# Three stages of an attention and expert layer: three blocks with barriers, or one block with waits by data

## The reference

```python
x = L0_attn_x                                   # (8, 512, 256)
xn = _layernorm(x)
# attention: 16 heads of 16, a band of 64 keys to either side
qkv = xn @ Wqkv + bqkv
scores = where(|i - j| <= 64, q @ k.T * 16 ** -0.5, -inf)
attn_out = softmax(scores) @ v @ Wout + bout
# experts: 8, hidden 1024, the top 2 of each token
logits = xn @ router_w + router_b               # gating: softmax over the top 2
h = relu(xn @ w1[e] + b1[e]);  y = h @ w2[e] + b2[e]
ffn_out = sum over the two experts of gating * y
out = x + attn_out + ffn_out
```

## Time and profile before

| | |
|---|---|
| median of 3 runs | 956.04 us (954.45 to 956.12) |
| the profiled execution's own time | 957.17 us |
| its span | 955.1 us |
| TensorE busy | 903.1 us (95%) |
| VectorE busy | 824.7 us (86%) |
| ScalarE busy | 740.7 us (78%) |
| GpSimd busy | 480.5 us (50%) |

### The profile page before, as it was taken

One profiled execution on the slowest core, in us unless ns is written; L12 is line 12 of the kernel. 1 busy time (PEld: TensorE's weight loads), 2 busy tenths in 40 slices (PEclk: granted clock), 3 DMA queues, 4 the chain that ended last, 5 costly groups with the idle time before them and its releaser, 6 DMA issues. The chain is left out here.

```text
span 955.1 us, 27555 instructions
## 1 busy us (share of the span) xinstructions
PE 903.1 (95%) x7684; PEld 876.4 (92%) x7684; DVE 824.7 (86%) x2171; ACT 740.7 (78%) x1985; POOL 480.5 (50%) x700
## 2 busy tenths in 40 slices
PE   4989799899999999999969999999999999999996
PEld 3878788889999999999969999999999999999996
DVE  5876699998888888888857999999999999999995
ACT  3545699899999999999956777777777776777773
POOL 5120013236465646555544666556666666556663
PEclk9999799999999999999998999999999999999999
DMA  4979532344444444455335222222222222221210
GB/s 143 322 268 308 169 79 75 117 122 136 136 136 135 137 135 133 136 141 148 105 87 163 37 34 44 46 36 36 34 34 43 47 49 49 35 44 35 36 22 1
DMA packets 69867, 95.33 MB, mean 100 GB/s; under 512 B 15549, under 2 KB 48960, under 8 KB 69696
## 3 DMA queue, kind: packets, MB, share of 16 engines
q1 hardware_dynamic: 52800, 77.97, 27.0%
q0 software_dynamic: 17024, 16.88, 11.2%
HBM read 62.91 MB, written 35.53 MB: 103 GB/s over the span
## 5 line engine op out<-in xcount | busy, mean ns | idle before, releaser
L1029 ACT ACTIVATE weights_qkv<-weights_qkv,low 128x256 f32<-128x256 f32 (+1 forms) x512 | 240.2, 480 | 1.1 <-DVE low L832 1.1
L1456 ACT ACTIVATE hid<-ps_experts,b_s 128x256 f32<-128x256 f32 x312 | 131.0, 473 | 117.5 <-PE ps_experts L1523 87.4
L1344 POOL DMA_INDIRECT out<-y,target x78 | 137.3, 1761 | 127.4 <-DVE y L1422 113.8
L843 DVE TENSOR_TENSOR pt<-ps_attend,pt 128x512 fp32r<-128x512 f32 (+1 forms) x256 | 158.4, 620 | 39.9 <-ACT pt L1042 39.3
L1123 PE MATMUL ps_attend<-pt,v_m 128*80 128x256 f32 (+7 forms) x1536 | 187.8, 271 | 2.3 <-DVE inv_t L856 1.8
L1539 PE MATMUL ps_experts<-w_hi,h_hi 128*128 128x256 f32 x624 | 175.4, 281 | 1.1 <-DVE h_lo L1391 1.1
L1523 PE MATMUL ps_experts<-xgt_hi,w_hi 128*128 128x256 f32 x624 | 173.7, 278 | 2.8 <-DVE xgt_lo L1382 2.8
L1123 PEld LDWEIGHTS ps_attend<-pt,v_m 128*80 128x80 f32 (+3 forms) x1536 | 171.4, 162 | 4.2 <-issue 4.2
L1523 PE MATMUL ps_experts<-xgt_hi,w_lo 128*128 128x256 f32 x624 | 173.6, 278 | 0.0
L1523 PE MATMUL ps_experts<-xgt_lo,w_hi 128*128 128x256 f32 x624 | 173.5, 278 | 0.0
L1539 PE MATMUL ps_experts<-w_lo,h_hi 128*128 128x256 f32 x624 | 172.6, 277 | 0.0
(11 more groups left out here) (174 smaller groups left out, 2008.6 us busy)
## 6 DMA issues: line engine op xcount, KB each, us to landing
weights_qkv<-in_w SPq DMA_DIRECT2D x15, 1024.0 KB, 7.1
qk_hi<-weights_qkv SPq DMA_DIRECT2D x16, 512.0 KB, 4.8
qk_lo<-weights_qkv SPq DMA_DIRECT2D x16, 512.0 KB, 5.5
q_st<-qk_hi SPq DMA_DIRECT2D x128, 64.0 KB
k_st<-qk_hi SPq DMA_DIRECT2D x128, 64.0 KB
weights_qkv<-in_x SPq DMA_DIRECT2D x8, 512.0 KB, 4.3
xn_rows<-weights_qkv SPq DMA_DIRECT2D x8, 512.0 KB, 5.2
k_st<-qk_lo SPq DMA_DIRECT2D x64, 64.0 KB
```

Of the source, the lines that this page charges most:

```text
L843: v.tensor_tensor(lo[:, f:l], ps[:, bank_t[h], 0:l - f], hi[:, f:l].bitcast(F32), ALU.subtract).then_inc(s_plo, 1)
L1029: ins = act.activation(wt[:, ring, at_tile(i)], wt[:, ring, at_tile(i)], ACT.Exp, bias=low[:, ring, i:i + 1], scale=-1.0, accum_out=total[ ...
L1344: pool.indirect_dma_start(out_tokens, bass.IndirectOffsetOnAxis(ap=target[:, h:h + 1], axis=0), y[:, h], None, bounds_check=T - 1, oob_is_ ...
L1456: ins = act.activation(hid[:, n % 2, j], ps[:, bank_h[n], j * ROWS:(j + 1) * ROWS], ACT.Relu, bias=b1[:, ds(e * FC + 2 * n + j, 1)])
```

## The change

All three stages stand in one block. There is no drain, barrier or `start` between them; the order at both seams is kept by waits on what is needed.

- Tiles of the later stages become views of F32R buffers that stay allocated: the parts of w1 lie in `q_st`, those of w2 in `v_m` and `k_st`, the projection's `w_lo` and `xt_lo`, attention's `pt` and the experts' rows and hidden layer share `work`, and so on.
- The semaphores of the later stages (65, and the two of the output stores) are raised by GpSimd at the start of the program.
- Seam 1: the scores of head 0 follow the projection; before those of head 1 TensorE waits for VectorE's last q and k part, behind those of head 2 for the logits. VectorE waits for the mask constants and the normalised rows' stores, GpSimd for v.
- Seam 2: GpSimd gathers the first rows after head 14 of the last batch. ScalarE and VectorE load the first expert's number and make w1's first half before the last inverses and values, ScalarE w1's second half after the inverses. TensorE runs the first half of the last projection, then waits for the gathered rows and transposes them, then runs the second half. The rows' parts, w1's second half on VectorE and w2's first half follow. The second and third gather each have their memset directly ahead; the third's waits for the second's landing.
- The identity is cast at the start of the program, b1 is loaded early in attention.

```diff
                                    base=0, pattern=[[-1, P]], channel_multiplier=1).then_inc(s_ident, 1)
+                start(pool, g.later.values())
+                start(pool, g.s_out)
...
+                v.wait_ge(s_ident, 2 + START)
+                v.tensor_copy(g.ident_r[:], g.ident[:])
                 statistics(0, 0)
...
-        pt = sb("pt", [P, 2, 2, SPAN], F32R)
-        a_hi = sb("a_hi", [P, DC, N], F32R)
-        a_lo = sb("a_lo", [P, DC, N], F32R)
+        pt = g.work[:].rearrange("p (r s w) -> p r s w", r=2, s=2)
+        a_hi, a_lo = g.split[:, 0], g.split[:, 1]
...
+                    sp.dma_start(g.b1[:], g.b1_cols).then_inc(s_b1, 16)
...
+                def gather_first():
+                    pool.wait_ge(s_rows, 16 + START)
+                    pool.tensor_copy(g.index[:, 0], g.rows[:, 0:2, 0].bitcast(U32)).then_inc(s_idx, 1)
+                    pool.wait_ge(s_idx, 1 + START)
+                    for h in range(2):
+                        pool.indirect_dma_start(
+                            g.first_rows[:, h].bitcast(F32), None, g.xn_dram,
+                            bass.IndirectOffsetOnAxis(ap=g.index[:, 0, h:h + 1], axis=0),
+                            bounds_check=T - 1, oob_is_err=False).then_inc(g.s_g[h], 16)
...
+                        if last and n == 14:
+                            gather_first()
+
+                pool.wait_ge(g.projection["s_vlo"], 2 * B + START)
                 batch(0, True, False)
                 batch(1, False, False)
+                pool.wait_ge(g.projection["s_table"], 16 + START)
                 with pool.Fori(2, B - 1) as b:
                     batch(b, False, False)
                 batch(B - 1, False, True)
-                pool.wait_ge(s_rows, 16 + START)
-                pool.tensor_copy(g.first_index[:], g.rows[:, 0:2, 0].bitcast(U32)).then_inc(s_first, 1)
-                pool.wait_ge(s_first, 1 + START)
-                for h in range(2):
-                    pool.indirect_dma_start(
-                        g.first_rows[:, h].bitcast(F32), None, g.xn_dram,
-                        bass.IndirectOffsetOnAxis(ap=g.first_index[:, h:h + 1], axis=0),
-                        bounds_check=T - 1, oob_is_err=False).then_inc(g.s_g[h], 16)
...
+                v.wait_ge(g.projection["s_const"], 5 + START)
+                v.wait_ge(g.projection["s_xnout"], 16 * B + START)
...
+                v.wait_ge(s_named, 1 + START)
+                first = v.value_load(g.step_expert[0:1, 0:1], min_val=0, max_val=E - 1)
+
+                def lo_of_w1(n):
+                    cols = slice(n * F // 2, (n + 1) * F // 2)
+                    v.wait_ge(s_w1hi, n + 1 + START)
+                    v.tensor_tensor(g.w1_lo[:, :, cols], g.w1_of(first)[:, :, cols], g.w1_hi[:, :, cols].bitcast(F32),
+                                    ALU.subtract).then_inc(s_w1lo, 1)
+
+                lo_of_w1(0)
                 v.wait_ge(s_pv, HC * 2 * B + START)
                 v.wait_ge(s_invs, 2 * B + START)
...
-                add_projected(B - 1, 0, bank_t[0])
-                add_projected(B - 1, 1, bank_t[1])
+                v.wait_ge(s_xhi, 1 + START)
+                v.tensor_tensor(g.xt_lo.rearrange("p c n -> p (c n)"), ps[:, bank_t[0], :],
+                                g.xt_hi.rearrange("p c n -> p (c n)").bitcast(F32), ALU.subtract).then_inc(s_xlo, 1)
+                for h in range(2):
+                    add_projected(B - 1, h, bank_last[h])
+                lo_of_w1(1)
+                half = slice(0, FC // 2)
+                v.wait_ge(s_w2hi, 1 + START)
+                v.tensor_tensor(g.w2_lo[:, half], g.w2_of(first)[:, half], g.w2_hi[:, half].bitcast(F32),
+                                ALU.subtract).then_inc(s_w2lo, 1)
 
...
+                act.wait_ge(s_wlast, 16 + START)
+                hi_of_w1(0)
                 inverse_out(2 * B - 1, False)
+                hi_of_w1(1)
                 act.wait_ge(s_proj, 2 * (B - 1) + START)
                 for h in range(2):
                     act.wait_ge(s_enda, h + 1 + START)
                     act.activation(a_hi[:, 1, half_of(h)], inv_t[:, half_of(h)], ACT.Copy).then_inc(s_endhi, 1)
+                act.wait_ge(s_tr4, 1 + START)
+                act.activation(g.xt_hi.rearrange("p c n -> p (c n)"), ps[:, bank_t[0], :], ACT.Copy
+                               ).then_inc(s_xhi, 1)
+                act.wait_ge(s_wload, 32 * (E - 1) + START)
+                half = slice(0, FC // 2)
+                act.activation(g.w2_hi[:, half], g.w2_of(first)[:, half], ACT.Copy).then_inc(s_w2hi, 1)
+                act.wait_ge(s_b1, 16 + START)
...
                 scores(0, 0, True)
+                pe.wait_ge(g.projection["s_qklo"], 4 * B + START + 1)
                 scores(0, 1, True)
                 scores(0, 2)
+                pe.wait_ge(g.projection["s_lgout"], B + START)
...
                 transpose_inverse(2 * B - 1)
                 weighted_values(B - 1, heads - 1)
+                for h in range(2):
+                    project(B - 1, h, range(0, 6), bank_last[h])
+                for h in range(2):
+                    pe.wait_ge(g.s_g[h], 16)
                 for c in range(DC):
                     for h in range(2):
-                        project(B - 1, h, range(6 * c, 6 * c + 6), bank_t[h])
+                        ins = pe.transpose(ps[:, bank_t[0], (c * 2 + h) * P:(c * 2 + h + 1) * P].bitcast(F32R),
+                                           g.gathered[0][:, h, c * P:(c + 1) * P], g.ident_r[:])
+                ins.then_inc(s_tr4, 1)
+                for h in range(2):
+                    project(B - 1, h, range(6, 12), bank_last[h])
...
-                for ring in range(1, RING):
-                    pool.memset(xg(ring)[:].bitcast(F32), 0.0).then_inc(s_xz, 1)
-                pool.wait_ge(s_xz, RING - 1 + START)
-                for h in range(2):
-                    pool.wait_ge(s_g[h], 16)
                 for n in range(1, RING):
+                    if n == 1:
+                        pool.wait_ge(s_s, DC * HC * B + START)
+                    else:
+                        pool.wait_ge(s_pv, DC * HC * B + START)
+                    pool.memset(g.gathered[n].bitcast(F32), 0.0).then_inc(s_xz, 1)
+                    pool.wait_ge(s_xz, n + START)
+                    for h in range(2):
+                        pool.wait_ge(s_g[h], 16 * n)
                     gather(n, n, n)
...
+        g.work = sb("work", [P, 4 * (6 * P + P)], F32R)
+        g.split = sb("split", [P, 2, DC, N], F32R)
+        g.w1_hi, g.w1_lo = (g.q_st[:, n * DC * F:(n + 1) * DC * F].rearrange("p (c f) -> p c f", c=DC)
+                            for n in range(2))
+        g.w2_hi = g.v_m[:].rearrange("p r h t d -> p (r h t d)").rearrange("p (m d) -> p m d", m=FC)
+        g.w2_lo = g.k_st[:].rearrange("p r a n -> p (r a n)").rearrange("p (m d) -> p m d", m=FC)
+        g.xt_hi, g.xt_lo, late_rows = (g.work[:, n * 2 * D:(n + 1) * 2 * D].rearrange("p (c n) -> p c n", c=2)
+                                       for n in range(3))
+        g.h_hi = g.work[:, 6 * D:6 * D + FC * ROWS].rearrange("p (m n) -> p m n", m=FC)
+        g.h_lo = g.split[:].rearrange("p s c n -> p (s c n)").rearrange("p (m n) -> p m n", m=FC)
+        g.gathered = (g.first_rows[:], g.q_st[:, 2 * DC * F:2 * DC * F + 2 * D].rearrange("p (h d) -> p h d", h=2),
+                      late_rows)
+        with nc.Block() as g.block:
             norm_project(nc, g)
             attend(nc, g)
-        experts(nc, g)
+            experts(nc, g)
```

More of the change, by code:

```diff
@@ L3 @@
 import math
-from contextlib import ExitStack
+from contextlib import ExitStack, nullcontext
 import concourse.bass as bass
@@ L98, in sem @@
             by[engine].append(ctx.enter_context(nc.semaphore(name)))
+            g.projection[name] = by[engine][-1]
             return by[engine][-1]
@@ L173, in v_tiles @@
             return ps[:, bank_v + 2 * n:bank_v + 2 * n + 2, 0:D].rearrange("p t (c d) -> p t c d", c=DC)
-        with nc.Block() as block:
+        with nullcontext(g.block) as block:
             @block.sync
@@ new lines, in attend @@
+        s_bias = sem("s_bias")
+        s_bo = sem("s_bo")
+        s_top = sem("s_top")
+        s_pick = sem("s_pick")
+        s_gap = sem("s_gap")
+        s_ratio = sem("s_ratio")
+        s_count = sem("s_count")
+        s_rank = sem("s_rank")
+        s_placed = sem("s_placed")
+        s_vm = sem("s_vm")
+        s_s = sem("s_s")
+        s_low = sem("s_low")
+        s_exp = sem("s_exp3")
+        s_t = sem("s_t")
+        s_phi = sem("s_phi")
+        s_plo = sem("s_plo")
+        s_pv = sem("s_pv")
@@ new lines, in attend @@
+        s_rec = sem("s_rec")
+        s_invt = sem("s_invt")
+        s_inv = sem("s_inv")
+        s_invs = sem("s_invs")
+        s_a = sem("s_a")
+        s_ahi = sem("s_ahi")
+        s_alo = sem("s_alo")
+        s_proj = sem("s_proj")
+        s_proj0 = sem("s_proj0")
+        s_done = sem("s_done")
```

(41 more changed lines are left out.)

193 lines of the change are left out of this document (65 added, 128 removed).

## The result

The changed kernel takes 964.51 us (median of 4 runs, 963.56 to 965.46), against 955.9 for the kernel before (4 runs beside it, 954.45 to 956.12): the ratio is 1.0093, with a 95% interval of 1.0077 to 1.0109. It is 8.6 us slower, where 12 us of gain were forecast. The profiled execution has a span of 963.7 us (965.46 with what lies around it).

A forecast was written before the change was run, and what follows sets the result against it. The prediction took gapless TensorE work behind the second seam to bound the kernel. Gains of 10.0 us there and 2.45 at the first seam sum to 12.45, from the median of 956.04 to 943.6 us; range 940.8 to 947.8.

The forecast's parts named there:

- Seam 1: Between projection and attention: without the barrier the first mask comes 2.45 us earlier, bounds 0 and 2.5.
- Seam 2: Between attention and experts: step 0 starts 7.1 us earlier and takes 2.9 us less, together 10.0 us.
- What bounds the kernel: Behind the second seam TensorE runs without a wait, 11.28 us a step, so an earlier step 0 shortens the whole.
- Edits at nothing: Program start, views instead of tiles, unchanged stage loops and the b1 load: all counted as costing nothing.
- Its own sentence for being wrong: Wrong if a step but the first is longer, TensorE awaits a landing in step 0, or attention loses its 2.45.
- the passage of the new waits: VectorE between its last logits sum and the first mask: counted at 0.05 us for the waits it passes.
- The table load: ScalarE's 1.28 us load ahead of attention's first exponential: would run from 98.61 to 99.9, hidden.
- the row stores: VectorE's new wait ahead of the first mask: counted as passed; if late, it costs up to 2.45 us.
- Rival (a): The clock stays up after the first seam: 2.2 us more gain, 941.4 us; chance 0.20.
- Rival (b): Second seam gives less: VectorE's subtraction holds GpSimd's copy (+1.2), the clock falls (2.9), or both: 944.8 to 947.7; chance 0.21.
- Rival (c): GpSimd's work behind a gather waits 5.5 us as the drain did, delaying head 15's values: 949.1; chance 0.04.
- Rival (d): Expert loop: GpSimd's chain lengthens each of 38 steps; slower from 0.38 us a step, 962.6 at 0.5; chance 0.03.

The follow-up runs named there:

- gap64: The changed kernel with 64 unused bytes per partition ahead of `work`; 943.87 us against 956.86 of the kernel before, ratio 0.9868.
- before_gap192: The kernel before with 192 unused bytes ahead of `more_rows`, moving rows and hidden parts to 192 modulo 256 like the weights; 977.26 us against 956.86.
- seam1_block: gap64 with `norm_project` in a block of its own again, so only the first seam has its drain and barrier; 946.15 us, ratio 0.989.
- gather_later: gap64 with the first rows' gather issued after head 15's inverse copy instead of after head 14's additions; 944.02 us, ratio 0.9873.
- seam2_block: gap64 with `experts` in a block of its own again, the order of the work ahead of it as in gap64; 950.4 us, ratio 0.9939.
- gap96: The changed kernel with 96 unused bytes ahead of `work`; 961.31 us.
- shift64: The changed kernel with 64 unused bytes ahead of `q_st`, so all five operand buffers shift and their distances stay; 963.89 us.
- gap128: The changed kernel with 128 unused bytes ahead of `work`; 959.38 us.
- gap192: The changed kernel with 192 unused bytes ahead of `work`; 951.46 us.
- gap32: The changed kernel with 32 unused bytes ahead of `work`; 955.16 us.
- places_before: The changed kernel with 192 unused bytes ahead of `q_st` and 64 ahead of `work`, giving the old kernel's operand places modulo 256; 951.2 us, ratio 0.9956.

## Why the prediction was wrong, step by step

**What bounds the kernel** was read rightly: behind the second seam the chain is TensorE without a wait. That is also why the miss is so large. Nothing covers a longer slot there: 96 slots by 0.0067 is 0.64 us a step by the slots alone, 0.59 in the chain, 21.9 us in 37 steps.

**The step that failed** stands under "Edits at nothing": "The views instead of tiles change no instruction's size, and the loops of the three stages keep their instructions." Both halves of the sentence are true, and the conclusion, a price of nothing, is wrong: the views changed where the operands lie to each other, from 192 apart to 0. The prediction gave this step no bounds and no rival; the range started at nothing for it. The trace of before has no second placement, so no row could have priced it; the addresses could have been compared, though, and that they all change was plain. Runs with an unused gap show the price: 20.6 us in the changed kernel (gap64), 20.4 in the old one (before_gap192). Its own sentence for being wrong, "if any step but the first is longer", is what happened.

**Seam 1**, counted at 2.45, came out at 2.1 (4.48 - 2.37). The part that was too small is the passage of the new waits: 0.40 us of VectorE between its last sum's end and the first mask, counted at 0.05. The table load was hidden (97.77 to 99.05), and the row stores were not late. seam1_block gets 1.0 of the 2.1 back by the block's end; the other 1.1 lie behind the old kernel's barrier, where its increments stand (what each of them costs was not tried).

**Seam 2**, counted at 10.0, came out at 10.5. From first mask to step 0 the old kernel took 502.99 - 102.17 = 400.82 us, the new one 393.16: 7.66, against 7.1 counted. Step 0 takes only 0.26 us more than the steps behind it, where it took 14.34 - 11.28 = 3.06 more: 2.8, against 2.9. TensorE's inverse transposes waited 1.36 us for the copy behind the gather. Counted from the first mask they start 0.98 us later than in the old kernel (387.80 against 386.82), where 1.6 were counted; that is the 0.6 by which step 0 comes earlier than forecast. The price of that order is real: gather_later takes it away, and pays it back as a wait for the landing. seam2_block shows the two parts of the seam by themselves, 4.0 and 2.5 us.

**Rival (a)**, a clock that holds at seam 1, came in part, and in some executions only. A stretch at 0.50 is there in every trace, but it lasts 10.2 us in after, gap64, seam1_block and gap96, and only 3.4 us in shift64, gap128, gap192, gap32 and places_before. From first mask to step 0 the first four take 393.2 to 393.7 us, the other five 390.8 to 391.4: the means are 2.2 us apart, the 2.2 that this rival counted. The four executions of after split in the same way, 963.56 and 963.63 us at a mean clock of 0.996, 965.40 and 965.46 at 0.993 to 0.994. What picks the length is not shown. That the clock stays low as long as before, which the forecast took, held in about half of the executions. **Rival (b)**: the clock part fell. The port was there, but in another place. GpSimd's copy had started 0.17 us before VectorE's subtraction, as counted, and took its usual 0.61; the additions behind it took 2.40 instead of 1.42 and the subtraction 1.54 instead of 1.23. Nobody waited for either. This is in the direction of the lock that the Trainium skill describes (SBUF — State Buffer, section "SBUF: two separate sides"), off the path. **Rival (c)**: GpSimd's memset starts right at the second gather's end (485.94), with no wait of 5.5 us. **Rival (d)** had the right place, a longer step in the expert loop, and the right arithmetic (over 0.38 us a step the kernel is slower), with the wrong cause: GpSimd still waits for y about as long, 100.8 us in 36 times between 520 and 940 us (2.8 each) beside 111.3 in 38 (2.9) in the earlier trace rows, and TensorE waits for nobody there.

**The sum.** Seam 1 and seam 2 together are 2.1 + 10.5 = 12.6 us, where 12.45 were counted. Step 1 starts 12.84 us earlier: besides the seams it has 0.86 us of a projection stage that ended earlier (96.83 against 97.69; between executions it differs as much), and it lacks the 0.59 by which step 0 is longer like all others. With the old slot, then, the kernel would take about what was forecast, and gap64, which has that slot from step 4 on, does: 943.87 us where 943.6 were forecast. That it is so exact is partly luck, since gap64 loses 1.4 us in its first steps and wins 1.2 in the projection stage (96.49).

## What to carry to other kernels

Where TensorE runs without a gap, the places of its two operands are part of the change: write down the address modulo 256 of the stationary and the moving tile before and after any edit to allocation, and look at the time from one matmul's start to the next; the busy share was 100% in both kernels and a matmul's length showed 0.28 us in both. If a tight loop becomes a few per cent slower with the same instructions and no waits, an unused gap of 64 bytes is a cheap thing to try early; the table shows that not every distance gives the time back. And a term that is counted at nothing because "the instructions are the same" needs a line of its own with a bound: here it was larger than all the others together.

## What the runs showed of the hardware that I had not expected

- The slot of a 128x256 F32R matmul at the full clock is 0.1133, 0.1178 or 0.1200 us by where the operands lie, in otherwise equal code, and for operands 64 bytes apart it can be in either of the first two for whole steps (gap64: three steps at 11.68 us, one at 11.47, then 11.27 to the end).
- GpSimd's drain at the second seam ends 5.4 us behind the end of GpSimd's last instruction: at 498.2 against 492.80, a gather, in the old kernel, and at 497.2 against 491.72 in seam2_block, where the last instruction is an addition and the last gather had ended at 488.34. At the first seam of both, with no gather ahead of it, it ends 0.1 us behind (81.35 against 81.24 in the old kernel). What it waits for is not shown.
- The stretch at the low clock behind seam 1 differs between executions: 10.2 us in after and gap64, 6.8 us in gather_later, 3.4 us in shift64 and gap192, though TensorE's work there is the same. The time from the first mask to the last matmul of attention follows it: 393.0 us in gap64, 390.8 in gap192. Differences of about 2 us between single executions of this kernel come from that.
